# The first attention's values prepared on POOL in three groups of source tiles in place of five

## What is computed

```python
xh = (x @ W).reshape(N, heads, out_c)
a_src = jnp.sum(xh * att_src, axis=-1)
a_dst = jnp.sum(xh * att_dst, axis=-1)
alpha = jax.nn.leaky_relu(a_src[src] + a_dst[dst], NEG_SLOPE)
...
e = jnp.exp(alpha - m[dst])
s = jax.ops.segment_sum(e, dst, num_segments=N)
coef = e / s[dst]
msg = xh[src] * coef[:, :, None]
out = jax.ops.segment_sum(msg, dst, num_segments=N)
```

## Time and profile before

| | us |
|---|---|
| median of three runs (2070.48 to 2072.76) | 2071.18 |
| the profiled execution | 2069.24 |
| its span in the trace | 2067.4 |
| the stage of the first attention's sum, from PE's first matmul to the last reduction's start | 884.2 to 1391.1 |
| one head of that stage | 63.6 |

### The profile page before, as it was taken

How to read it: one execution, slowest core, us unless ns; L and a number is a source line. 1 busy time by engine, 2 the same in 40 slices (tenths; PEclk the granted TensorE clock), 3 DMA queues, 4 the chain that set the end, 5 groups by cost and what they waited for, 6 DMA issues and landing times. The chain is left out here.

```text
span 2067.4 us, 56651 instructions
## 1 busy us (share of the span) xinstructions
PE 1640.1 (79%) x23014; PEld 1482.0 (72%) x23014; DVE 1481.0 (72%) x2364; ACT 1232.5 (60%) x1981; POOL 886.1 (43%) x559
## 2 busy tenths in 40 slices
PE   4599999964388882378888888881499799999996
PEld 1599999953376761377778777771499788898895
DVE  6788989834577774389999999984688644444545
ACT  1355666521255551298889988881367566666665
POOL 0699999801445542098888877700000000000000
PEclk9799999986699996589999999995799999999998
DMA  1100000002111211311110011103300000000001
GB/s 57 41 14 13 15 14 13 14 7 80 52 34 50 55 52 29 76 32 42 43 42 27 22 42 43 38 3 103 97 26 13 24 20 12 3 1 3 16 1 52
DMA packets 82632, 68.24 MB, mean 33 GB/s; under 512 B 21630, under 2 KB 74001, under 8 KB 82273
## 3 DMA queue, kind: packets, MB, share of 16 engines
q1 hardware_dynamic: 79047, 62.01, 10.4%
q0 software_dynamic: 3328, 2.56, 0.7%
HBM read 47.36 MB, written 17.19 MB: 31 GB/s over the span
## 5 line engine op out<-in xcount | busy, mean ns | idle before, releaser
L2251 ACT ACTIVATE branch_mask<-branch_row,att_att 128x3126 bf16<-128x3126 f32 (+1 forms) x208 | 461.0, 2289 | 46.5 <-DMA branch_row<-dst_row 38.7
L2564 PE MATMUL sage_acc<-sage_cr,sage_hl 128*128 128x448 f32 x1750 | 378.5, 372 | 10.3 <-DVE sage_hl L2680 10.3
L497 POOL DMA_INDIRECT swp_slab<-records,e_rows x100 | 314.4, 3144 | 89.7 <-POOLq L120 55.9
L2564 PEld LDWEIGHTS sage_acc<-sage_cr,sage_hl 128*128 128x128 f32 x1750 | 324.1, 189 | 35.7 <-DVE sage_hl L2680 10.4
L2328 PE MATMUL branch_acc<-branch_v,branch_mask 128*128 128x102 bf16 (+1 forms) x5000 | 299.7, 214 | 61.9 <-DVE branch_mask L2278 37.5
L2284 DVE TENSOR_TENSOR branch_mask<-branch_mask,k_C 128x3126 bf16<-128x3126 bf16 (+1 forms) x208 | 312.6, 1550 | 17.2 <-ACT branch_mask L2251 16.3
L2590 ACT ACTIVATE sage_cr<-k_C 128x896 fp32r<-128x896 bf16 x250 | 235.2, 945 | 146.8 <-PE sage_acc L2564 142.7
L2328 PEld LDWEIGHTS branch_acc<-branch_v,branch_mask 128*128 128x128 bf16 (+1 forms) x5000 | 256.7, 100 | 87.9 <-DVE branch_mask L2278 41.5
L2650 DVE CAST sage_cr<-k_C 128x896 fp32r<-128x896 bf16 x250 | 128.6, 515 | 207.2 <-PE sage_acc L2564 207.2
L2517 POOL TENSOR_TENSOR sage_xr<-sage_xr,sage_b 128x640 f32<-128x640 f32 x5 | 7.7, 1551 | 470.4 <-DMA sage_xr<-x 470.4
L419 PE MATMUL swp_pw<-swp_hot,swp_low_hot 128*128 128x100 bf16 x1568 | 198.9, 217 | 12.9 <-DVE swp_hot L413 9.8
(11 more groups left out here) (297 smaller groups left out, 2902.4 us busy)
## 6 DMA issues: line engine op xcount, KB each, us to landing
branch_row<-dst_row SPq DMA_DIRECT2D x24, 384.0 KB
mean_feat<-in_edge_attr SPq DMA_DIRECT2D x50, 144.0 KB, 2.2
branch_row<-dst_row SPq DMA_DIRECT2D x8, 411.0 KB
table<-lin_tab SPq DMA_DIRECT2D x5, 340.0 KB, 5.9
branch_tab<-table SPq DMA_DIRECT2D x8, 212.5 KB
att_sums<-branch_mask SPq DMA_DIRECT2D x8, 212.5 KB, 2.3
post_sums<-att_sums SPq DMA_DIRECT2D x5, 340.0 KB, 3.2
table<-lin_tab SPq DMA_DIRECT2D x5, 322.5 KB, 2.4
```

The source lines that it names most:

```text
L497: pool.indirect_dma_start(slab[:, t % 2, j * ROW:(j + 1) * ROW, :].rearrange("p e f -> p (e f)"), None, k.records, bass.IndirectOffsetOnAx ...
L2251: nc.scalar.activation(mask[:, slot(e, s), cols(lo, hi)], row[:, cols(lo, hi)], ACT.Relu, bias=g.att[:, 1, bass.ds(h + s * heads, 1)], sca ...
L2564: ins = pe.matmul(acc[:, bank, 0:hi - lo], hl[:, part, g % RING, :], cr[:, n % CR_SLOTS, lo - first:hi - first], start=g == 0 and part == ...
```

## The change

The source tiles form three groups, 0 to 8, 9 to 16 and 17 to 24. The table is fetched group by group into a buffer for one group, in place of one for all tiles: each load waits for the first operation (L2217) of the group before it, by `v_chain`. SP issues the next head's three loads in a row, each with its wait, ahead of the row loads. The buffer `rest` grows to nine tiles. POOL gets the wait for the load inside the loop over groups, and one no-op more. POOL's arithmetic stays the same for each tile.

```diff
--- before.py
+++ after.py
@@ -89,7 +89,7 @@
 ON_DVE, ON_ACT = (0, 3), (1, 2)
 GROUPS = 3
 CHUNKS = ((0, 6), (6, 12), (12, 18), (18, TILES))
-V_PARTS = tuple((lo, lo + PERIOD) for lo in range(0, TILES, PERIOD))
+V_PARTS = ((0, 9), (9, 17), (17, TILES))
 
 
 assert CW >= N_NODES and TILES % STRIP == 0 and RP * RE >= N_EDGES + SLOTS * ROW
@@ -2107,8 +2107,8 @@
         row = m.sb("row", [P, LIVE], F32)
         mask = m.sb("mask", [P, MASKS, LIVE], BF16)
         v = m.sb("v", [P, TILES, 3, 3, w1], BF16)
-        rest = m.sb("rest", [P, V_PARTS[0][1], 2, w1], F32)
-        tab = m.sb("tab", [P, TILES, w1], F32)
+        rest = m.sb("rest", [P, max(hi - lo for lo, hi in V_PARTS), 2, w1], F32)
+        tab = m.sb("tab", [P, max(hi - lo for lo, hi in V_PARTS), w1], F32)
         low = m.sb("low", [P, TILES // PERIOD, heads], F32)
         acc = m.ps("acc", [P, 8, BANK])
         row_in, tab_in, stored = [m.sem(f"row_in{x}") for x in range(len(CHUNKS))], m.sem("tab_in"), m.sem("stored")
@@ -2171,9 +2171,10 @@
                         sp.dma_start(row[:, at], g.dst_row[bass.ds(h, 1), at].rearrange("a n -> (a n)")
                                      .partition_broadcast(P)).then_inc(row_in[x], 16)
 
-                    def load_tab(h):
-                        sp.dma_start(tab[:, :, :], g.table[bass.ds(h, 1)].rearrange("a p t c -> p (a t) c")
-                                     ).then_inc(tab_in, 16)
+                    def load_tab(h, n):
+                        lo, hi = V_PARTS[n]
+                        sp.dma_start(tab[:, 0:hi - lo, :], g.table[bass.ds(h, 1), :, lo:hi, :]
+                                     .rearrange("a p t c -> p (a t) c")).then_inc(tab_in, 16)
 
                     def store(e, h):
                         sp.wait_ge(added, h + 1)
@@ -2181,9 +2182,10 @@
                                      ).then_inc(stored, 16)
 
                     def next_head(e, h):
-                        sp.wait_ge(v_ready, h * len(V_PARTS))
-                        sp.nop(nofuse=True)
-                        load_tab(h)
+                        for n in range(len(V_PARTS)):
+                            sp.wait_ge(v_chain, h * (len(V_PARTS) * 6) + ((n - 1) * 6 + 1))
+                            sp.nop(nofuse=True)
+                            load_tab(h, n)
                         sp.wait_ge(masked, h * MASKED + (masked_upto[last_direct + 1] - MASKED))
                         for x in range(len(CHUNKS)):
                             sp.wait_ge(raised, h * RAISED + (raised_upto[LAST] + x + 1 - RAISED))
@@ -2192,9 +2194,12 @@
                         store(1 - e, h - 1)
 
                     sp.sem_inc(stored, 16)
-                    load_tab(0)
+                    load_tab(0, 0)
                     for x in range(len(CHUNKS)):
                         load_row(0, x)
+                    for n in range(1, len(V_PARTS)):
+                        sp.wait_ge(v_chain, (n - 1) * 6 + 1)
+                        load_tab(0, n)
                     next_head(1, 1)
                     with sp.Fori(1, heads // 2) as u:
                         for e in (0, 1):
@@ -2208,13 +2213,14 @@
                     pool.wait_ge(parts_ready, 1)
                     with pool.Fori(0, heads) as h:
                         link = Chain(pool, v_chain, h * (len(V_PARTS) * 6))
-                        pool.wait_ge(tab_in, h * 16 + 16)
-                        for lo, hi in V_PARTS:
+                        for n, (lo, hi) in enumerate(V_PARTS):
+                            pool.wait_ge(tab_in, h * (len(V_PARTS) * 16) + (n * 16 + 16))
                             pool.wait_ge(tiles_done, h * TILES + hi)
+                            pool.nop(nofuse=True)
                             r, of = rest[:, 0:hi - lo], v[:, lo:hi, 0:2]
                             share = g.att[:, 0:5:4, :].rearrange("p x (t h) -> p t x h", h=heads)
                             shape = [P, hi - lo, 2, w1]
-                            link(pool.tensor_tensor(r, tab[:, lo:hi, :].unsqueeze(2).broadcast_to(shape),
+                            link(pool.tensor_tensor(r, tab[:, 0:hi - lo, :].unsqueeze(2).broadcast_to(shape),
                                                     share[:, lo:hi, :, bass.ds(h, 1)].broadcast_to(shape), ALU.mult))
                             for part in (0, 1):
                                 pool.nop(nofuse=True)
```

## The result

| | before | after |
|---|---|---|
| median of five runs, us | 2071.38 (2070.48 to 2075.92) | 2083.9 (2079.69 to 2085.47) |
| profiled execution (its span), us | 2069.24 (2067.4) | 2079.69 (2077.9) |

The medians differ by 12.5 us; the forecast was 2083.5 us. After to before, taken over all runs, is 1.0051 with a 95% interval of 1.0037 to 1.0066, which is 10.6 us.

The account below looks back on a forecast made before the run. A ring of ACT, DVE and PE, hanging on mask 22's end, bounds each head. 11.9 - 0.6 + 1.0 + 0.3 = +12.6 us on 2069.24 gives 2081.8; the median lies 1.94 higher: 2083.5, range 2071 to 2089.

Parts of the forecast that it names:

- The ring and its room: First attention's sum: ACT, DVE and PE release each other, mask 22 sets the head; DVE can lose 0.99 us per five tiles.
- The price by elements read: DVE masks behind POOL operations: excess grows with elements POOL reads, about 0.001 us an element less 0.05.
- Mask 22: DVE's direct mask of tile 22 in each head: ends 1.96 us later than with POOL silent.
- the term of 11.9: Mask 22 ending 1.7 us later than before, in seven heads that have a next one to prepare: +11.9 us.
- Early tiles: Tiles before tile 8 are free of POOL, so ACT's break of 0.39 on PE goes: -0.6 us.
- Group 2 beside the reductions: At a head's end, POOL's work on tiles 17 to 24 delays DVE's additions by 0.15 a head: +1.0 us.
- Head 0: First head: its share of mask 22's delay (1.7), plus +0.3 us for a start delay mostly covered by PE's wait on DVE.
- No growth: Rival: a DVE mask's excess does not grow with the POOL operation; +0.7, 2071.9; chance 0.18 together with another phase.
- POOL leaving the late tiles: Rival: seven heads end like the last, POOL-silent head, and ACT's waits for PE go; -3.0, 2068.2; chance 0.05.
- SP's queue: Table loads ahead of row loads cost nothing; rival, SP holds the row loads back: 2085 to 2095, chance 0.01.
- the prediction's 10 us: SP's last table load goes out after group 1's first operation, which ends 10 us before the row loads are issued.
- DVE held for the whole operation: Rival: DVE is blocked for a POOL operation's whole length; mask 22 4.9 us late, +33, 2104; chance 0.03.

Follow-up runs that it names:

- e9_last_group_later: The changed kernel with POOL starting a head's last group only after DVE's first mask piece of the next head; ratio 1.0076 to the kernel before.
- e3_half_reads: The changed kernel with both subtractions of a group replaced by copies of the remainder onto itself, halving their reads; ratio 1.0018 to the kernel before.
- e8_split_subtractions: The changed kernel with each subtraction issued as two instructions of half the tiles, total reads the same; ratio 1.0042 to the kernel before.
- e7_five_narrow: The changed kernel with groups of five tiles, keeping its one-group table buffer and load waits; ratio 1.0184 to the kernel before.
- the second series: The changed kernel measured again, unaltered, against the kernel before in the same series; ratio 1.0074 (1.0061 to 1.0087).
- e2_five_split: The changed kernel with groups of five tiles, table still fetched by group but into a buffer for all tiles; ratio 1.0022 to the kernel before.

## Why the prediction came out

**The ring and its room:** right. Heads 1 to 6 grew by 1.65 us each on average, the last head not at all, and the idle time before tiles 16 and 21 is gone in the former and there in the latter. (Head 1 keeps 0.52 before tile 21, after a wait of ACT on PE of 1.72.) One sentence was too strong, that what DVE loses early is free as long as it comes to tile 21 before ACT: in the last head of `e9_last_group_later` it does, and mask 22 is 0.70 us late all the same, by way of PE and ACT at tile 8.

**The price by elements read:** right, also past the last row on which it stood. Predicted for nine tiles 0.27, 0.57 and 0.42, measured 0.24, 0.56 and 0.37; for eight tiles 0.23 and 0.50 for CAST and TENSOR_TENSOR, measured 0.21 and 0.47 to 0.50; on direct masks 0.51 and 0.44, measured 0.50 and 0.43. The halved reads of `e3_half_reads` and the split ones of `e8_split_subtractions` fall on the same line. An f32 copy (306 reads) and a bf16 TENSOR_SCALAR (459 reads, fewer bytes) stand in the order of their elements.

**Mask 22:** 1.96 us later than with POOL silent, measured 51.89 - 49.99 = 1.90. The order was right too: tile 17 spared (3.46), tile 18 the first of the second group. The difference to before was put at 1.7. In before, mask 22 of head 3 came 50.60 after ACT's resumption, 0.61 later than silent, of which 0.19 is lost by ACT before tile 8 and 0.42 is DVE's, where the prediction had 0.26. So DVE's difference is 1.48: the term of 11.9 is 10.4 by that.

```profile
1128.52 3.71 DVE L2278 SCALAR_TENSOR_TENSOR branch_mask<-branch_row,branch_low,k_C 128x3126 bf16<-128x3126 f32 x1
```

**Early tiles:** 0.6 over all heads, measured 0.19 in head 3 alone. ACT's waits on PE at tile 8 are gone; in their place it waits at tiles 18 and 23 (0.52 and 0.27 in the rows above), where DVE is later than ACT anyway.

**Group 2 beside the reductions:** 0.15 a head, measured 0.20 in head 3 (1.15 + 0.69 against 1.04 + 0.60); a further 0.14 lies between the last addition's end and ACT's resumption, on the store, a stretch that differs by up to 0.63 between the heads of one trace (2.24 to 2.87 in before).

**Head 0:** wrong in both its halves, which nearly cancel. It was to grow by its share of mask 22 (1.7) and 0.3 for a later start. From ACT's first mask to tile 8 it became 2.07 shorter, and from there to mask 22 3.18 longer (42.06 against 38.88): there POOL prepares head 0's later groups and then head 1's almost without a pause, the masks are lengthened from tile 3 on, and DVE has no idle time from there to tile 24. The early gain is told below. Head 0 gave +1.06 in place of about +2, and this makes over half of the distance between 12.6 predicted for the stage and 11.0 measured.

**The rivals.** No growth, and POOL leaving the late tiles, fell with the masks above. SP's queue cost nothing here, for the reason given, but in `e7_five_narrow`, where POOL falls behind in every head, it costs 39 us (2107.16 against 2068.19). The queue costs time once POOL's product comes after mask 22. In the change the last table load is out 11 us before that mask's end, so the prediction's 10 us were about right. DVE held for the whole operation, the rule of the Trainium skill's "SBUF — State Buffer", section "Who interferes with whom": the TENSOR_SCALAR above ends at 1119.93, 1.33 us into a mask that grew by 0.37. The trace does not agree with the length that the rule gives.

The total is right to 0.4 us partly by luck: the stage gave 1.6 less than the sum, and the medians differ by 1.5 more than the stage. By the ratio over all runs the change costs 10.6 us, where the forecast lies 12.3 over its 2071.18. What the medians have beyond the stage, and why the second series stood at 0.74%, was not found. Its profiled execution has 12.1 us in the stage, and head 6 alone accounts for more than the 1.1 between the two series: there PE's granted clock was 0.54 in 1334.40:1337.80, right behind mask 22, and from that mask's end to the last addition it took 11.39 us in place of 9.94. Outside the stage the ten profiled executions take 1551.6 to 1558.3 us, whatever the edit.

## What to carry to other kernels

Fewer instructions are no gain where an engine works in the shadow of another. Ask what each one makes the other lose, and whether the loss falls inside the room between two waits or beyond it: the sum over one such stretch decides, not the busy time. Before a load is hung on another engine's progress, see whether that engine keeps step in the stretch (operations a group against slots a group), and what stands behind the load in its queue. A single silent repetition in the trace, here the last head, gives the room and the price without any experiment.

## What was not expected of the hardware

The first table load of the change is 9/25 of the old one and stands ahead of the row loads in SP's queue. ACT's second piece of the row came after a wait of 0.25 us in place of 1.57. PE's clock differs too. Windows of before, then after, with the columns of the earlier trace rows; the number behind POOL's busy time, ahead of the DMA share, is the granted clock, 0.50 being 1.2 GHz and 1.00 2.4 GHz:

```profile
885.00:888.50 3.50, 3.11 (x37) 2.31 (x34) 2.00 (x3) 3.46 (x4) 2.92 (x5) 0.50 0.06 23
888.50:892.00 3.50, 1.61 (x30) 1.41 (x30) 2.12 (x2) 3.50 (x2) 3.28 (x4) 0.50 0.00 0
892.00:896.00 4.00, 4.00 (x57) 3.62 (x56) 4.00 (x2) 4.00 (x3) 3.79 (x3) 0.50 0.00 0
```

```profile
885.00:888.50 3.50, 3.26 (x50) 3.13 (x50) 1.53 (x1) 3.50 (x2) 3.15 (x5) 0.50 0.10 24
888.50:892.00 3.50, 3.50 (x78) 3.23 (x76) 3.50 (x2) 3.50 (x2) 3.42 (x2) 0.77 0.01 3
892.00:896.00 4.00, 3.69 (x82) 3.21 (x79) 4.00 (x3) 4.00 (x3) 3.71 (x3) 1.00 0.02 4
```

Before, PE starts at 884.19, stands still for 1.89 us behind a late mask and is at the lower level to 896; after, it starts at 885.24, has no such break, and is at the higher level throughout the third window. ACT's wait of 0.80 on PE at tile 8 is gone with it.

That the early gain belongs to the fetch in pieces and not to the wider groups is shown by `e2_five_split`, which has groups of five: from ACT's first mask to tile 8 it takes 18.17 us, the change 18.08 and before 20.15, and PE's granted clock in 888.50:892.00 is 1.00. All nine traces in which the first load is a part lie between 17.8 and 18.6. That the small load lets the row pieces land sooner is argued and not shown, and of before there is one trace alone.
